# Both feed-forward phases of a macaron block as unrolled pipelines over chunks, with two buffers, the first normalisation on GpSimd and the down projection one chunk behind

## The reference, cut to what matters

```
x = x + 0.5 * ffn(layernorm(x), w_gate, w_up, w_down)      # phase A, first part
x = x + attention(layernorm(x), W1, b1, W2, b2, Wg, bg, Wo, bo)
x = x + 0.5 * ffn(layernorm(x), w_gate, w_up, w_down)      # phase D

ffn(y):  gate = y @ wg.T; up = y @ wu.T                     # int weights / 127, hidden 384
         return (silu(gate) * up) @ wd.T
attention(y): h = silu(y @ W1.T + b1) @ W2.T + b2; qkv = h @ Wg.T + bg
         16 heads of 64, key j masked where j >= i + 64, softmax, @ v, @ Wo.T + bo
```

## Time and profile before

| | us |
|---|---|
| median of 3 runs | 1632.81 (1631.2 to 1634.49) |
| the profiled execution, its own time | 1628.43 |
| its span, first to last instruction | 1626.6 |
| TensorE busy | 1439.0 (88%) |
| GpSimd busy | 990.7 (61%) |
| VectorE busy | 970.6 (60%) |
| ScalarE busy | 776.3 (48%) |
| mean granted TensorE clock | 0.976 of full speed |

### The profile page before, as it was taken

One profiled execution on the slowest core, in us unless ns is written; L12 is line 12 of the kernel. 1 busy time (PEld: TensorE's weight loads), 2 busy tenths in 40 slices (PEclk: granted clock), 3 DMA queues, 4 the chain that ended last, 5 costly groups with the idle time before them and its releaser, 6 DMA issues.

```text
span 1626.6 us, 38540 instructions
## 1 busy us (share of the span) xinstructions
PE 1439.0 (88%) x13330; PEld 1113.7 (68%) x13330; DVE 970.6 (60%) x1886; ACT 776.3 (48%) x1827; POOL 990.7 (61%) x592
## 2 busy tenths in 40 slices
PE   4767999999999999999999999999999999998676
PEld 3543777777777777777777777777777777777566
DVE  5653666666666666566666656666666656665444
ACT  2323555555555455554555555555555455454332
POOL 2231767677666667666676766677666666667410
PEclk9995999999999999999999999999999999999978
DMA  3100000000000000000000000000000000000000
GB/s 96 36 0 18 19 19 19 18 18 18 18 18 18 13 5 18 18 18 18 18 18 18 18 18 18 18 18 18 18 18 18 18 1 17 18 0 1 1 26 26
DMA packets 30571, 29.42 MB, mean 18 GB/s; under 512 B 6993, under 2 KB 25298, under 8 KB 30546
## 3 DMA queue, kind: packets, MB, share of 16 engines
q1 hardware_dynamic: 30546, 29.09, 5.9%
HBM read 8.07 MB, written 2.10 MB: 6 GB/s over the span
## 4 chain that ended last, share of the span: by engine, by line
PE 55%; issue 17%; DVE 13%; POOL 7%; ACT 6%; DVEq 1%; DMA 1%; ACTq 0%; POOLq 0%; SPq 0%
PE banks L773 16%; PE banks L754 15%; PE banks L789 8%; PE banks L719 6%; POOL probs L324 6%; ACT probs L389 5%; DVE probst L549 4%; DVE negmax L537 4%; PE banks L655 4%; PE banks L742 2%; PE banks L723 2%; DVE hidden L492 1%; PE banks L734 1%; POOL rstd_ln L295 1%; DVE xn_ln L478 1%
## 5 line engine op out<-in xcount | busy, mean ns | idle before, releaser
L324 POOL TENSOR_SCALAR probs<-probs,recips 128x704 f32<-128x704 f32 (+7 forms) x512 | 947.6, 1864 | 452.5 <-DVE recips L542 452.5
L537 DVE TENSOR_REDUCE negmax<-banks 128x1 f32<-128x704 f32 (+7 forms) x512 | 392.6, 808 | 129.8 <-PE banks L754 129.8
L773 PE MATMUL banks<-ident,probs 128*128 128x128 f32 x2752 | 391.4, 281 | 43.2 <-DVE probst L549 22.6
L397 ACT ACTIVATE probst<-banks 128x512 f32<-128x512 f32 (+1 forms) x320 | 177.4, 555 | 516.2 <-PE banks L773 516.2
L389 ACT ACTIVATE probs<-banks,negmax 128x704 f32<-128x704 f32 (+7 forms) x512 | 397.2, 785 | 44.5 <-DVE negmax L537 44.5
L773 PEld LDWEIGHTS banks<-ident,probs 128*128 128x128 f32 x2752 | 293.2, 141 | 130.3 <-issue 69.3
L549 DVE COPY probst<-banks 128x512 f32<-128x512 f32 (+1 forms) x416 | 276.6, 665 | 171.8 <-PE banks L773 169.8
L789 PE MATMUL banks<-probst,vs 128*64 128x128 f32 x5504 | 357.0, 277 | 0.8 <-ACT probst L397 0.8
L789 PEld LDWEIGHTS banks<-probst,vs 128*64 128x64 f32 x5504 | 295.3, 137 | 37.6 <-issue 22.5
L754 PE MATMUL banks<-kt,qt 64*128 64x512 f32 (+4 forms) x2496 | 298.3, 365 | 3.1 <-issue 3.1
L754 PEld LDWEIGHTS banks<-kt,qt 64*128 64x128 f32 x2496 | 206.0, 186 | 50.5 <-issue 5.8
(11 more groups left out here) (58 smaller groups left out, 881.1 us busy)
## 6 DMA issues: line engine op xcount, KB each, us to landing
hslot<-h_sb SPq DMA_DIRECT2D x32, 512.0 KB, 3.2
wslot<-in_wqkvt SPq DMA_DIRECT2D x32, 128.0 KB, 3.0
wslot<-wq_sb SPq DMA_DIRECT2D x32, 64.0 KB, 2.6
y<-xres SPq DMA_DIRECT2D x8, 256.0 KB, 2.3
wo_sb<-in_wot SPq DMA_DIRECT2D x1, 512.0 KB
wq_sb<-in_wqkvt SPq DMA_DIRECT2D x1, 512.0 KB
bslot<-bqk_sb SPq DMA_DIRECT2D x32, 1.0 KB, 1.9
iload<-in_wgatet SPq DMA_DIRECT2D x1, 192.0 KB, 2.4
```

Source lines behind the costliest of these rows:

```text
L324: nc.gpsimd.tensor_scalar(here, here, recips[:, c, h:h + 1], None, ALU.mult).then_inc(normed.sem, 1)
L397: nc.scalar.activation(probst[c % 2][:, 4 * g:4 * g + w, :].rearrange("p t q -> p (t q)"), banks[:, TRANSPOSED[g % 2], 0:w * P], ACT.Copy) ...
L537: nc.vector.tensor_reduce(negmax[:, c, h:h + 1], src, AX.X, ALU.max, negate=True).then_inc(maxed.sem, 1)
L773: last = nc.tensor.transpose(banks[:, TRANSPOSED[g % 2], (t - 4 * g) * P:(t - 4 * g + 1) * P], probs[c, h][:, kb * P:(kb + 1) * P], ident[:])
```

## The change

Both feed-forward phases become one Python-unrolled program `feed_forward(ph)` per engine. Chunk numbers are constants, so there is no hardware loop and no address in a register. `xth`, `hidden`, the ln1 `xn` and `stats` get two buffers, `mv` and `rstd` three. The two `hidden` buffers are views of `probst`, which only the attention stage uses otherwise; `bvx` becomes a view of `vs[0]`. The four ln1 normalisation instructions of a chunk move from VectorE to GpSimd, two chunks ahead of their use; ln1 statistics run three chunks ahead. The down projection and the residual of chunk t-1 run in iteration t, the ln2 layernorm and the first small matmul of chunk t-2 in iteration t, the second small matmul of chunk t-3 in iteration t. The transposition of ln2 (t-2) stands in the middle of down (t-1). The loads of x become three: chunk 0 (0.25 MB) ahead of the integer weights, then chunk 1, then chunks 2 to 7 (1.5 MB). `low(ph, 0)` now follows the statistics of chunks 0, 1 and 2. The core of the diff:

```diff
-        xth = sb("xth", [P, 2, CH], F32R)
+        xth = [sb(f"xth{k}", [P, 2, CH], F32R) for k in range(2)]
-        hidden = sb("hidden", [P, HB, CH])
+        hidden = [probst[k][:].rearrange("p t q -> p (t q)")[:, 0:HB * CH].rearrange("p (j n) -> p j n", j=HB) for k in range(2)]
-        bvx = probst[0][:, 0:PAIRS, :]
+        bvx = vs[0]
...
+        def done(eng, tally, event, t):
+            if t >= 0:
+                eng.wait_ge(tally.sem, tally.after(event, t))
...
@@ sync
+            x_parts = [slice(0, CT), slice(CT, 2 * CT), slice(2 * CT, TOK // P)]
+            sp.dma_start(resident[:, x_parts[0], :], x_src[:, x_parts[0], :]).then_inc(x_loaded[0], 16)
             for dst, src in ((iload[:, 0:HID], wgatet), (iload[:, HID:2 * HID], wupt),
...
+            for k in (1, 2):
+                sp.dma_start(resident[:, x_parts[k], :], x_src[:, x_parts[k], :]).then_inc(x_loaded[k], 16)
...
@@ gpsimd
+            def layernorm(ph, t):
+                done(pool, ph.rstd["ln1"], "r", t)
+                done(pool, ph.tr["ln1"], "t", t - 2)
+                pool.sem_inc(idle, 1)
+                for k in range(CT):
+                    nc.gpsimd.tensor_scalar(xn["ln1"][t % 2][:, k, :], xres[:, t * CH + k * D:t * CH + (k + 1) * D], mv["ln1"][t % 3][:, k, 0:1],
+                                            rstd["ln1"][t % 3][:, k:k + 1], ALU.subtract, ALU.mult).then_inc(ph.norm["ln1"].sem, 1)
...
+            def feed_forward(ph):
+                for t in range(3):
+                    rstd_of(ph, "ln1", t)
+                    if t < 2:
+                        layernorm(ph, t)
...
+                for t in range(CHUNKS + 2):
+                    if ph is pa and 0 <= t - 2 < CHUNKS:
+                        rstd_of(pa, "ln2", t - 2)
+                    if t + 2 < CHUNKS:
+                        layernorm(ph, t + 2)
+                    if ph is pa and 0 <= t - 2 < CHUNKS:
+                        add_bias(t - 2)
+                    if t + 3 < CHUNKS:
+                        rstd_of(ph, "ln1", t + 3)
...
@@ scalar
+            def feed_forward(ph):
+                copy_transposed(ph, "ln1", 0)
+                for t in range(CHUNKS + 3):
+                    if t < CHUNKS:
+                        silus(ph, t)
...
+                    if ph is pa and 0 <= t - 3 < CHUNKS:
+                        hidden_state(t - 3)
+                    if t + 1 < CHUNKS:
+                        copy_transposed(ph, "ln1", t + 1)
+                    if ph is pa and 0 <= t - 2 < CHUNKS:
+                        copy_transposed(pa, "ln2", t - 2)
+                        inner(t - 2)
...
@@ vector
+            def feed_forward(ph):
+                for t in range(3):
+                    if ph is pa:
+                        dve.wait_ge(x_loaded[t], 16)
+                    statistics(ph, "ln1", t)
+                    if t == 0 and ph is pa:
+                        dve.wait_ge(ints_loaded, 16 * 3)
...
+                low(ph, 0)
...
+                for t in range(CHUNKS + 2):
+                    if t < CHUNKS:
+                        gate(ph, t)
+                    if ph is pa and 0 <= t - 2 < CHUNKS:
+                        layernorm2(t - 2)
+                    if t + 1 < CHUNKS:
+                        low(ph, t + 1)
+                    if t + 3 < CHUNKS:
+                        statistics(ph, "ln1", t + 3)
+                    if 0 <= t - 1 < CHUNKS:
+                        residual(ph, t - 1)
+                        if ph is pa:
+                            statistics(pa, "ln2", t - 1)
...
@@ tensor
+            def down(ph, t):
+                done(pe, ph.hid, f"h{HB - 1}", t)
+                done(pe, ph.x1, "x", t - 1)
                 for k in range(CT):
                     for j in range(HB):
...
+                    if k == 1 and ph is pa and 0 <= t - 1 < CHUNKS:
+                        transposed(pa, "ln2", t - 1)
+                last.then_inc(ph.down.sem, 1)
...
+                for t in range(CHUNKS + 3):
+                    if t < CHUNKS:
+                        gate_up(ph, t)
...
+                    if ph is pa and 0 <= t - 3 < CHUNKS:
+                        outer(t - 3)
+                    if t + 1 < CHUNKS:
+                        transposed(ph, "ln1", t + 1)
+                    if 0 <= t - 1 < CHUNKS:
+                        down(ph, t - 1)
+                    elif ph is pa and 0 <= t - 2 < CHUNKS:
+                        transposed(pa, "ln2", t - 2)
+                    if ph is pa and 0 <= t - 2 < CHUNKS:
+                        inner(t - 2)
```

More of the change, by code:

```diff
@@ L309, in _ @@
[L309 to L317, removed]
+                nc.gpsimd.tensor_scalar(veps[ln][:], mv[ln][t % 3][:, :, 1], EPS, None, ALU.add).then_inc(ph.rstd[ln].sem, 1)
@@ L363, in _ @@
[L363 to L374, removed]
+                    done(act, ph.gu, f"g{j}", t)
@@ L443, in _ @@
                     take(tc, 3, ti)
[L445 to L449, removed]
+            feed_forward(pd)
         @block.vector
@@ L470, in statistics, with layernorm2 @@
                 for k in range(CT):
[L471 to L476, removed]
+                    nc.vector.bn_aggr(mv[ln][t % 3][:, k, :], stats[ln][t % 2][:, k, :]).then_inc(ph.stat[ln].sem, 1)
+            def layernorm2(t):
+                done(dve, pa.tr["ln2"], "t", t - 1)
+                done(dve, pa.rstd["ln2"], "r", t)
@@ L510, in _ @@
-            nc.vector.tensor_scalar(wq_sb[:], wq_sb[:], DH ** -0.5, None, ALU.mult).then_inc(bq_scaled, 1)
-            gate(pa, 0)
-            low(pa, 1)
-            residual(pa, 0, 0)
-            with dve.Fori(1, CHUNKS - 1) as t:
-                at_last, at, at_next = dve.snap((t - 1) * CH), dve.snap(t * CH), dve.snap((t + 1) * CH)
-                statistics(pa, "ln2", t - 1, at_last)
-                statistics(pa, "ln1", t + 1, at_next)
-                layernorm(pa, "ln2", t - 1, at_last)
-                layernorm(pa, "ln1", t + 1, at_next)
-                gate(pa, t)
-                low(pa, t + 1)
-                residual(pa, t, at)
@@ L523, in _ @@
-            t = CHUNKS - 1
-            statistics(pa, "ln2", t - 1, (t - 1) * CH)
-            layernorm(pa, "ln2", t - 1, (t - 1) * CH)
-            gate(pa, t)
-            residual(pa, t, t * CH)
-            statistics(pa, "ln2", t, t * CH)
-            layernorm(pa, "ln2", t, t * CH)
-            dve.wait_ge(pa.biased.sem, pa.biased.after("b", CHUNKS - 1))
+                    last = nc.vector.tensor_scalar(xn["ln2"][0][:, k, :], xres[:, t * CH + k * D:t * CH + (k + 1) * D], mv["ln2"][t % 3][:, k, 0:1],
+                                                   rstd["ln2"][t % 3][:, k:k + 1], ALU.subtract, ALU.mult)
@@ new lines, in layernorm2, with low, gate @@
+                last.then_inc(pa.norm["ln2"].sem, 1)
+            def low(ph, t):
+                done(dve, ph.copied["ln1"], "c", t)
+                done(dve, ph.gu, f"u{HB - 1}", t - 2)
+                nc.vector.tensor_tensor(xth[t % 2][:, 1, :], banks[:, T_BANK["ln1"], :], xth[t % 2][:, 0, :], ALU.subtract).then_inc(ph.xlo.sem, 1)
+            def gate(ph, t):
+                for j in range(HB):
+                    done(dve, ph.silu, f"g{j}", t)
+                    done(dve, ph.gu, f"u{j}", t)
+                    done(dve, ph.down, "d", t - 2)
+                    nc.vector.tensor_tensor(hidden[t % 2][:, j, :], gated[:, j, :], banks[:, 1 + HB + j, :], ALU.mult).then_inc(ph.hid.sem, 1)
@@ L668, in _ @@
-            transposed(pa, "ln1", 0)
-            pe.wait_ge(weights_ready, 2)
-            gate_up(pa, 0)
-            pe.wait_ge(pa.silu.sem, pa.silu.after("g0", 0))
-            transposed(pa, "ln1", 1)
-            pe.wait_ge(loaded, 16 * 9)
-            pe.wait_ge(consts, 2)
-            pe.wait_ge(bvx_ready, PAIRS)
-            for g in range(PAIRS):
-                mm(banks[:, WORK, 0:P], bvx[:, g, :], wo_sb[:, g, :], start=(g == 0), stop=False)
-            mm(banks[:, WORK, 0:P], ones_row[:], bo_row[:], start=False, stop=True).then_inc(bo_done, 1)
@@ L679, in _ @@
-            down(pa, 0)
-            pe.wait_ge(bo_done, 2)
-            with pe.Fori(1, CHUNKS - 1) as t:
-                gate_up(pa, t)
-                pe.wait_ge(pa.h.sem, pa.h.before("h", t - 1))
-                transposed(pa, "ln2", t - 1)
-                mlp1(t - 1)
-                pe.wait_ge(pa.silu.sem, pa.silu.after("g0", t))
-                transposed(pa, "ln1", t + 1)
-                down(pa, t)
-                mlp2(t - 1)
-            t = CHUNKS - 1
-            gate_up(pa, t)
```

236 lines of the change are left out of this document (105 added, 131 removed).

## The result

| | before | after |
|---|---|---|
| median of the runs, us | 1632.38 | 1682.67 (1679.97 to 1683.44) |
| ratio | | 1.0304, 95% interval 1.0286 to 1.0321 |
| span of the profiled execution | 1626.6 | 1681.1 |
| phase A (to the first projection) | 127.03 | 99.49 |
| attention | 1403.5 | 1516.7 |

The prediction said 1581.5 and faster; the kernel is 3% slower. Both edited phases became shorter, by 27.5 and 31.2 us. The attention stage, in which no line was changed, became 113.2 us longer: -27.5 - 31.2 + 113.2 = +54.5, the difference of the spans.

The account below looks back on a forecast made before the run. A serial round through VectorE and GpSimd was taken to bound each feed-forward chunk. Phase A -21.8 and phase D -29.4 make -51.2 us: 1577.2 profiled, 1581.5 against the median (4.4 higher); range 1571 to 1602, the forecast's own 1573 to 1588.

Parts of the forecast that it names:

- the first paragraph: Whole kernel: attention stays at 1403.5 us; only phase A (127 us) and phase D (96.1 us) can move.
- Bound and mechanism: Phases A and D: a serial round through VectorE and GpSimd bounds each chunk; after the change TensorE is the bound.
- the serial round: Phases A and D: each chunk's chain leaves TensorE for VectorE and GpSimd, 12.2 us a chunk in A, 11.95 in D.
- TensorE's need per chunk: Phases A and D: TensorE's summed work at full clock, 9.13 us a chunk in A and 6.43 in D.
- Lock: Phase A: GpSimd's normalisation makes VectorE's ln2 normalisation wait once a chunk, some 1.0 us; TensorE stands 0.2 to 0.5.
- The 0.4 us a chunk: Phase A: TensorE's stand for the lock, given as 0.2 to 0.5 us, with 9.5 us a chunk taken against 9.13.
- The rival with the lock in every instruction: Phase A: each of four ln2 normalisations waits for GpSimd, 10.9 us a chunk, 1590 us in all; chance 0.27 (1588 to 1602).
- GpSimd's normalisation: Phases A and D: four ln1 normalisations on GpSimd take 2.4 us, upper end 4.8, against 1.11 on VectorE.
- Phase A: First feed-forward phase: ends at 105.2 us instead of 127.03, -21.8 us, with gate_up(0) at 14.9 and 9.5 a chunk.
- the tail: End of phase A: from the last residual to the phase's end, kept as before at 12.1 us.
- Phase D: Last feed-forward phase: ends at 1597.2 us instead of 1626.6, -29.4 us, with 6.43 us a chunk.
- Clock: Phases A and D: TensorE's clock stays near 1.00; the rival has it fall to 0.50, 1657 us, chance 0.04.

Follow-up runs that it names:

- 64 increments: Kernel after with 64 semaphore increments that nothing waits for at the start of TensorE's program: 1569.62 us, ratio 0.9612 to the kernel before.
- run 15: Not a follow-up run: part of the words "a loop run 15 times", which mean the 15 iterations of TensorE's attention loop.
- +96: Kernel before with 96 semaphore increments at the start of TensorE's program, moving its attention loop by 96 places: 1663.81 and 1679.16 us.

## Why the prediction was wrong

The sum of its two phases was right in sign and a little low; the step that failed is the first paragraph: "The change edits nothing in that stage, so its 1403.5 us ... stay". It measured 1516.7. A stage's time was taken as a property of its lines, but here it is also one of where those lines lie in TensorE's program: at its new place the loop was fetched again each of the fourteen times that it went back, with 70 us more of idle TensorE and 43 us more of matmuls at the lower clock. 64 increments ahead of it brought the stage back to 1405.3. The prediction named its own check ("if attention's length moves by over 3 us, I am wrong about what is outside the edit"), but gave that no chance and no rival. The page of before held the number from which one could have started: 15 packets of instructions in all, for a loop run 15 times, meant that the loop stayed loaded, and the diff moves it by 489 instructions. What the place would cost stood nowhere in that page.

Point by point:
- **Bound and mechanism.** Right: the serial round is gone, TensorE is busy 8.10 of 8.10 us.
- **TensorE's need per chunk.** 9.13 and 6.43 predicted, 8.07 and 5.92 measured. The recorded durations of matmuls in a line contain the overlap with the next ones: the second small matmul is recorded with 1.02 us, but the transposition behind it starts 0.86 after it; a down has 2.68 in the chain where the timeline of before had 2.96, its value behind a wait. The sum must go from start to start.
- **Lock.** The 0.4 us a chunk did not come (downs 8.07 apart with TensorE busy throughout). VectorE's 32 ln2 normalisations after:

```profile
L499 DVE TENSOR_SCALAR xn_ln<-xres,mv_ln,rstd_ln x32: 341/342/440, 36.7 to 91.6; 128x128 f32<-128x128 f32 x32
```

  (minimum, median and maximum in ns.) None took over 0.1 us longer than the median, though GpSimd's normalisations ran beside them. The rival with the lock in every instruction was wrong.
- **GpSimd's normalisation.** 2.4 us for four predicted, between 2.4 and 4.8; measured 3.13. TensorE hid it in all but the first chunk.
- **Phase A.** -21.8 predicted, -27.5 measured: 1.4 us a chunk over five chunks less than assumed (9.5 against 8.07) make 7. Against that gate_up(0) came 1.9 late (16.80 against 14.9), because the last part of x landed at 14.79 and not at 12.7; by gate_up(3) 0.7 of it was left (40.28 against 39.6), and the tail was 0.8 longer.
- **Phase D.** -29.4 predicted, -31.2 measured. The first gate_up came 8.8 us behind the statistics (1616.16 to 1624.97), where 8.2 were predicted.
- **Clock.** Full in both phases' steady parts, as said; it fell in attention, where the rival had not looked, behind each stall (0.948 over the run, 0.976 before).

With the loop at a fast place the same change gives 1569.6 us, 12 under the prediction and just below its range. 5.7 + 1.8 of these are the two phases. The other 4.4 are the step from the profiled execution to the median: it was carried over from the kernel before, and the kernel after with 64 increments doesn't have it (1569.36 profiled, 1569.62 median).

## What to carry to other kernels

A change that adds or removes instructions ahead of a long hardware loop can change the time of the loop. Look at the instruction queue's packets on the page of before and after: if the loop is fetched again in each iteration, shift it by some tens of cheap instructions at a place where the engine waits anyway, and only then judge the change. How many depends on the place: here 32 and 64 did it and 192 did not, and from 96 on the kernel before became slower by them. A difference between two kernels with such a loop is not evidence for or against the edit until both have been seen at a fast place.

For a pipeline: put the normalisation and statistics ahead, give the buffers that they need a second copy, and the engine that does them matters little as long as TensorE is the bound; here one run shows it for the first normalisation.

## What was not expected of the hardware

- The attention stage, with the same loop of 1701 instructions, took 1403 to 1406 or 1489 to 1517 us by its place alone; being fetched again cost 6 to 8 us each time (83.5 to 113.2 over 14). Part of that is the clock, 0.50 for some microseconds behind each stall.
- At one place (+96) one kernel had two times, 1663.81 and 1679.16 us, and its loop was fetched again in five of fourteen iterations of the first, not before 700 us. Why it holds in the others is open.
- The kernel after had a second stall per iteration, and the others not. The end of a block 17 or 18 instructions behind the loop's head would explain it; no run was made for it.
- VectorE's normalisation waited 1.0 us for GpSimd's bias add (two tensors read), but not for GpSimd's normalisation (one tensor and two columns). The Trainium skill (SBUF — State Buffer, the rules on the shared port pair) has the second one block fully until the first is through, for a VectorE instruction of the kind that waits; on VectorE's side that was seen here for the bias add alone. On GpSimd's side one normalisation took 1.40 us instead of 0.79, beside a VectorE scaling of 0.68 us (line 537, kernel after). Back on VectorE, one ln1 normalisation took up to 0.99 us instead of 0.34, beside the bias add.
- A semaphore increment takes TensorE 0.155 us (first transposition at 22.9 us with 128 of them, at 42.8 with 256).
